# Attention output in token order by transfers, and the softmax denominators by small transfers of their own

## The reference, cut to what matters

```python
out = jnp.einsum('bnqk,bnkh->bnqh', attn, v)      # b, head n, query q, channel h
out = out.reshape(B, -1, S)                       # 256 x 256: the reshape mixes q, h and n
x = x + jnp.einsum('bds,nhd->bsd', out, W_out)    # = out[b, d, s] * sum over n, h of W_out[n, h, d]
```

## Time and profile before

| | |
|---|---|
| median of three runs | 965.46 us (962.29 to 969.97) |
| the profiled execution | 962.93 us |
| its span | 961.2 us |
| mean granted clock of TensorE | 0.967 |
| TensorE busy (PE) | 887.1 us, 92% of the span |
| VectorE, ScalarE, GpSimd busy | 586.2, 487.4, 496.3 us |
| chain that ended last: PE, VectorE, ScalarE, DMA, SP's queue | 80%, 7%, 5%, 2%, 2% |

### The profile page before, as it was taken

How to read it: one execution, slowest core, us unless ns; L and a number is a source line. 1 busy time by engine, 2 the same in 40 slices (tenths; PEclk the granted TensorE clock), 3 DMA queues, 4 the chain that set the end, 5 groups by cost and what they waited for, 6 DMA issues and landing times.

```text
span 961.2 us, 31757 instructions
## 1 busy us (share of the span) xinstructions
PE 887.1 (92%) x11966; PEld 653.0 (68%) x11966; DVE 586.2 (61%) x1292; ACT 487.4 (51%) x839; POOL 496.3 (52%) x705
## 2 busy tenths in 40 slices
PE   5999999999997689899998988999999999999995
PEld 3667667667665356565564776778888888878783
DVE  4856766766764456777777657455555555555552
ACT  3667677677666367566455542333333333333331
POOL 2556666566565333366666667534444434444432
PEclk9999999999999799999888899999999999999998
DMA  9222443443445654455453233433332333233322
GB/s 283 70 57 67 93 129 90 96 127 90 92 119 121 172 183 132 146 177 179 144 162 118 90 86 89 87 62 51 48 51 47 53 49 52 46 52 52 47 34 23
DMA packets 133197, 92.96 MB, mean 97 GB/s; under 512 B 75712, under 2 KB 114112, under 8 KB 132928
## 3 DMA queue, kind: packets, MB, share of 16 engines
q1 hardware_dynamic: 119760, 73.10, 28.2%
q0 software_dynamic: 13296, 17.83, 11.1%
HBM read 54.65 MB, written 37.32 MB: 96 GB/s over the span
## 4 chain that ended last, share of the span: by engine, by line
PE 80%; DVE 7%; ACT 5%; issue 3%; DMA 2%; SPq 2%; another core or an unknown queue 1%; POOL 0%; DVEq 0%; ACTq 0%; POOLq 0%
PE pair L933 19%; PE pair L949 12%; PE pair L951 6%; PE pair L634 5%; PE pair L671 5%; PE pair L657 4%; PE pair L811 3%; PE pair L607 3%; PE pair L684 2%; PE pair L825 2%; PE pair L829 2%; PE pair L861 2%; PE pair L900 2%; PE pair L786 1%; PE pair L837 1%
## 5 line engine op out<-in xcount | busy, mean ns | idle before, releaser
L933 PE MATMUL pair<-XTs,WU 128*128 128x128 bf16 x3408 | 283.9, 219 | 5.9 <-DVE XTs L1269 2.9
L933 PEld LDWEIGHTS pair<-XTs,WU 128*128 x3408 | 238.1, 98 | 71.7 <-issue 8.7
L1603 POOL DMA_INDIRECT out_d<-XB x71 | 116.1, 1635 | 207.4 <-DVE XB L1291 174.0
L949 PE MATMUL pair<-WD,Hh 128*128 x568 | 214.8, 379 | 1.3 <-issue 1.3
L1469 ACT ACTIVATE Hf<-pair 128x512 f32<-128x512 f32 x142 | 84.8, 597 | 219.5 <-PE pair L933 207.9
L1282 DVE CAST Hh<-Hf 128x512 bf16<-128x512 f32 x142 | 64.5, 454 | 172.1 <-ACT Hf L1469 166.9
L951 PE MATMUL pair<-WD,Hl 128*128 x568 | 154.7, 272 | 0.0
L1284 DVE TENSOR_TENSOR Hl<-Hf,Hh 128x512 bf16<-128x512 f32 x142 | 99.5, 701 | 4.9
L1514 POOL TENSOR_SCALAR_AFFINE_SELECT PT<-PT 128x512 f32<-128x512 f32 (+1 forms) x96 | 73.9, 787 | 44.2 <-ACT PT L1320 28.7
L1576 POOL DMA_INDIRECT xs_scr<-XB,WGf x64 | 66.9, 1045 | 31.7 <-issue 18.2
L1488 POOL TENSOR_TENSOR LS<-LS,mhalf 128x2 f32<-128x2 f32 x48 | 34.1, 711 | 94.6 <-DVE LS L976 93.9
(11 more groups left out here) (243 smaller groups left out, 1728.9 us busy)
## 6 DMA issues: line engine op xcount, KB each, us to landing
XB<-xs_scr SPq DMA_DIRECT2D x71, 130.0 KB
STG<-wup_in SPq DMA_DIRECT2D x32, 256.0 KB
q_scr<-SPL SPq DMA_DIRECT2D x16, 512.0 KB, 4.2
STG<-wdn_in SPq DMA_DIRECT2D x32, 256.0 KB
o_scr<-On SPq DMA_DIRECT2D x32, 128.0 KB, 4.2
Mm<-o_scr SPq DMA_DIRECT2D x16, 256.0 KB, 3.0
CnT<-ctxt_in SPq DMA_DIRECT2D x16, 256.0 KB, 4.0
CX<-ctx_in SPq DMA_DIRECT2D x16, 256.0 KB, 4.4
```

The source lines that it names most:

```text
L933: t = e.matmul(upb(j, k)[:, 128 * (fm % 4):128 * (fm % 4) + 128], WU[:, bass.ds(reg[j] * 4096 + off, 128)], XTs[:, r, hx, dk, :], start=n ...
L949: e.matmul(yb[r][:, 0:512], Hh[:, r, hsl], WD[:, bass.ds(reg[i] * 4096 + 512 * fk, 512)], start=fk == 0, stop=False, skip_group_check=True)
L1603: e.indirect_dma_start(out=out, out_offset=bass.IndirectOffsetOnAxis(ap=XS[:, i % NX, 256:257].bitcast(I32), axis=0), in_=Yf[:, i % NY, :] ...
```

## The change

- A4, X1's transposes and their PSUM user go away on TensorE. The projection's heads are laid out anew so that partition group j holds heads 4j to 4j+3 (`places` in layout, `c` in PV).
- ScalarE's copy of PV to OTs now writes the order (s', g, d'), reading PSUM in that permuted order.
- SP (step OT) issues one transfer of the denominators' rows from OTs to a small tile dnc, and four of 16 partitions that write the undivided output to DRAM in token order. XA reads it back, 256 KB, with tokens on partitions.
- VectorE (step RC) takes the reciprocal of dnc and multiplies by wsq. SP (step WB) writes this factor to DRAM with four transfers, and BC reads it back with two, each repeated over the 16 tokens that share it, as XR.
- VectorE (step X1, vector_residual) multiplies XA by XR and adds x.
- The orders change with it: X1 and A6s stand between S1's and S0's maxima on VectorE, A6s behind T0's first masks on GpSimd, and in SP's list the two loads of a round come behind XA.

```diff
 ROUND = {
-    "tensor": "AX:1 MG:1 S1:0:0 T0:1:0 PV:2 S1:0:1 QK:-1 T0:1:1 S0:0 VX:0 T2:1 GT:15 weights:1:2 A4:2",
-    "vector": "Gp:16 weights:-2:0 A6s:4 weights:-1:1 S1:0:1 S0:0 VX:0 A4:2 weights:1:2 MG:0 AX:0 S1:-1:0 Gs:15 A0s:-3",
+    "tensor": "AX:1 MG:1 S1:0:0 T0:1:0 PV:2 S1:0:1 QK:-1 T0:1:1 S0:0 VX:0 T2:1 GT:15 weights:1:2",
+    "vector": "Gp:16 weights:-2:0 weights:-1:1 S1:0:1 X1:4 A6s:4 S0:0 RC:2 weights:1:2 MG:0 AX:0 S1:-1:0 Gs:15 A0s:-3",
     "scalar": "PV:2 A0n:-2 QK:-1 T0:1:1 Gt:13 A6c:4 weights:-2:0 A6n:4 VX:0 T2:1 weights:-1:1 AX:0 GT:15 MG:0 T0:0:0",
-    "gpsimd": "weights:0:2 split:0 T0:1:0 T0:1:1 split:0 GT:15 T2:1 A6c:4 A0s:-3 A6s:3",
-    "sync": "GT:15 load:0 A4:3 AX:1 Go:16 queries:16 decays:16",
+    "gpsimd": "weights:0:2 split:0 T0:1:0 A6s:4 T0:1:1 split:0 GT:15 T2:1 A6c:4 A0s:-3",
+    "sync": "GT:15 BC:3 AX:1 OT:2 WB:2 XA:2 load:0:0 load:0:1 Go:16 queries:16 decays:16",
 }
...
+        def vector_denominators(e, w, b):
+            w.wait_ge(l_dc, 16 * (b + 1))
+            w.wait_ge(l_wb, 64 * b)
+            e.reciprocal(dnc[:, :], dnc[:, :]).then_inc(dvc.sem, dvc.up())
+            w.wait_ge(dvc.sem, dvc.n)
+            e.tensor_tensor(rc[:, :], dnc[:, :], wsq[:, :], ALU.mult).then_inc(rc_.sem, 1)
+
+        def vector_residual(e, w, b):
+            r = b % 2
+            w.wait_ge(l_xa[r], 16 * (b // 2 + 1))
+            w.wait_ge(l_bc, 32 * (b + 1))
+            e.tensor_tensor(XA[:, r, :, :], XA[:, r, :, :], XR[:, :, :], ALU.mult).then_inc(dvc.sem, dvc.up())
+            w.wait_ge(dvc.sem, dvc.n)
+            e.tensor_tensor(xb(b), XA[:, r, :, :], xb(b), ALU.add).then_inc(x1_.sem, 1)
...
                 elif kind == "PV":
                     w.wait_ge(pv.sem, pv.at(b))
-                    w.wait_ge(wsq_, 2)
-                    w.wait_ge(oT.sem, oT.at(b - 1))
-                    e.activation(OTs[:, :, :], pair_of("PV", b)[:, :, :].rearrange("p a (r c) -> p (a r) c", r=2), ACT.Copy).then_inc(ot_.sem, 1)
+                    w.wait_ge(wsq_, 1)
+                    w.wait_ge(l_ot, 64 * b)
+                    w.wait_ge(l_dc, 16 * b)
+                    e.activation(OTs[:, :, :].rearrange("p g c -> p (g c)").rearrange("p (s g d) -> p s g d", s=16, g=4),
+                                 pair_of("PV", b)[:, :, :].rearrange("p a (r d s) -> p s (a r) d", r=2, s=16), ACT.Copy).then_inc(ot_.sem, 1)
...
-                elif kind == "A4":
-                    w.wait_ge(on_.sem, on_.at(b))
+                elif kind == "OT":
+                    w.wait_ge(ot_.sem, ot_.at(b))
+                    w.wait_ge(rc_.sem, rc_.at(b - 1))
+                    e.dma_start(dnc[:, :], OTs[16:128:32, :, :].rearrange("p g c -> p (g c)").rearrange("p (s c) -> p s c", c=32)).then_inc(l_dc, 16)
+                    ov = osc[b, :].rearrange("(s h d) -> h s d", s=16, h=16)
+                    for j in range(4):
+                        e.dma_start(ov[:, :, 64 * j:64 * j + 64], OTs[32 * j:32 * j + 16, :, :].rearrange("p g c -> p (g c)").rearrange(
+                            "p (s c) -> p s c", s=16)).then_inc(l_ot, 16)
+                elif kind == "XA":
+                    w.wait_ge(l_ot, 64 * (b + 1))
+                    w.wait_ge(x1_.sem, x1_.at(b - 2))
+                    e.dma_start(XA[:, b % 2, :, :], osc[b, :].rearrange("(t p d) -> p t d", t=2, p=128)).then_inc(l_xa[b % 2], 16)
+                elif kind == "WB":
+                    w.wait_ge(rc_.sem, rc_.at(b))
+                    for j in range(4):
+                        e.dma_start(rsc[b, :].rearrange("(s j k c) -> j s k c", s=16, j=4, k=2)[j], rc[32 * j:32 * j + 32, :]).then_inc(l_wb, 16)
+                elif kind == "BC":
+                    w.wait_ge(l_wb, 64 * (b + 1))
+                    w.wait_ge(x1_.sem, x1_.at(b - 1))
                     for tt in range(2):
-                        e.dma_start(osc[b, :].rearrange("(n t p h) -> t p n h", n=NH, t=2, h=16)[tt], On[:, tt, :, :]).then_inc(l_o, 16)
-                    if b < B - 1:
-                        merged(e, w, b)
+                        e.dma_start(XR[:, tt, :], rsc[b, 2048 * tt:2048 * tt + 2048].rearrange("(s a d) -> s a d", s=8, a=1).broadcast_to(
+                            [8, 16, 256])).then_inc(l_bc, 16)
...
```

More of the change, by code:

```diff
@@ L74 @@
 ROUND = {
[2 rows of a table removed]
[2 rows of a table added]
     "scalar": "PV:2 A0n:-2 QK:-1 T0:1:1 Gt:13 A6c:4 weights:-2:0 A6n:4 VX:0 T2:1 weights:-1:1 AX:0 GT:15 MG:0 T0:0:0",
[2 rows of a table removed]
[2 rows of a table added]
 }
 LIMITS = {"S1": (0, B - 1), "T0": (0, B - 1), "PV": (0, B - 2), "A0s": (0, B - 1), "A0n": (0, B - 1), "QK": (0, B - 1), "A6s": (0, B - 4),
[L83 removed]
+          "A6n": (0, B - 4), "S0": (0, B - 1), "VX": (0, B - 1), "T2": (0, B - 1), "A6c": (0, B - 4), "X1": (0, B - 4), "OT": (0, B - 2), "XA": (0, B - 2),
+          "RC": (0, B - 2), "WB": (0, B - 2), "BC": (0, B - 2), "AX": (-2, B), "MG": (0, B)}
 def words(line):
@@ L115, in attn_steps @@
     yield "MG", B + 1, 0
-    yield "A4", B - 1, 0
+    yield "OT", B - 1, 0
     yield "contexts", 0, 0
+    yield "queries", 1, 0
+    yield "WB", B - 1, 0
+    yield "XA", B - 1, 0
     yield "decays", 1, 0
-    yield "queries", 1, 0
     yield "contexts", 1, 0
+    yield "BC", B - 1, 0
 def attention_rest():
     z = B - 1
-    return {(0, 0): (("A6s", z - 2), ("Mm", z), ("X1", z - 1), ("A6n", z - 2), ("A6c", z - 2)),
+    return {(0, 0): (("X1", z - 2), ("A6s", z - 2), ("RC", z), ("X1", z - 1), ("A6n", z - 2), ("A6c", z - 2)),
             (0, 1): (("A6s", z - 1), ("XQ", z - 2), ("A6n", z - 1), ("A6c", z - 1)), (0, 2): (("X1", z), ("A6s", z)),
@@ L281, in build @@
         OTs = sb("OTs", [128, 4, 256], F32, ca)
[L282 to L285, removed]
+        dnc = sb("dnc", [128, 32], F32, ca)
+        rc = sb("rc", [128, 32], F32, ca)
+        wsq = sb("wsq", [128, 32], F32, ca)
+        XA = sb("XA", [128, 2, 2, 256], F32, ca)
+        XR = sb("XR", [128, 2, 256], F32, ca)
         QN = sb("QN", [128, 2, 256], F32, ca)
@@ L394, in build @@
         t2m, ex2, pt2 = (sig(n, [(b, u) for b, _ in of(pe_attn, "T2") for u in range(2)]) for n in ("t2m", "ex2", "pt2"))
-        pv, ot_, oT, on_, mT, x1_ = (sig(n, each) for n in ("pv", "ot_", "oT", "on_", "mT", "x1_"))
-        l_o, l_m = sem("l_o"), [sem("l_m0"), sem("l_m1")]
+        pv, ot_, rc_, x1_ = (sig(n, each) for n in ("pv", "ot_", "rc_", "x1_"))
+        l_ot, l_dc, l_wb, l_bc, l_xa = sem("l_ot"), sem("l_dc"), sem("l_wb"), sem("l_bc"), [sem("l_xa0"), sem("l_xa1")]
         qn_, qT, qnh, qnl, ch_, cl_ = (sig(n, each) for n in ("qn_", "qT", "qnh", "qnl", "ch_", "cl_"))
@@ L519, in build @@
         EPS = 5e-5
-        tb_users = [s[:2] for s in pe_steps if s[0] in ("X1", "XQ", "GA", "GT", "GE", "B4", "B5")]
+        tb_users = [s[:2] for s in pe_steps if s[0] in ("XQ", "GA", "GT", "GE", "B4", "B5")]
         def tb_free(w, kind, b):
@@ L677, in tensor_attn @@
                     ps = pair_of("VX", b)
[L678 to L690, removed]
-                        for dk in range(2):
[L692 to L703, removed]
+                    w.wait_ge(wql, 2)
+                    for tt in range(2):
+                        n = 0
+                        for dk in range(2):
+                            for wt, v in ((WQh, xTh), (WQl, xTh), (WQh, xTl)):
+                                t = e.matmul(ps[:, 0, 256 * tt:256 * tt + 256], v[:, b % 2, dk, 128 * tt:128 * tt + 128], wt[:, dk, 512:768],
+                                             start=n == 0, stop=n == 5, skip_group_check=True)
+                                n += 1
+                    t.then_inc(vmm.sem, 1)
                 elif kind == "AX":
@@ L999, in vector_weights @@
             w.wait_ge(wsqm, 1)
[L1000 to L1006, removed]
+            selv = CF[:, C_SEL:C_SEL + 8].rearrange("p (k a) -> p k a", a=1).broadcast_to([128, 8, 32])
+            e.tensor_tensor(wtmp.rearrange("p (k c) -> p k c", c=32), pair_of("weights", 2)[:, 0, 0:256].rearrange("p (k c) -> p k c", c=32),
+                            selv, ALU.mult).then_inc(dvc.sem, dvc.up())
+            w.wait_ge(dvc.sem, dvc.n)
+            e.tensor_reduce(wsq[:, :], wtmp.rearrange("p (k c) -> p c k", c=32), AX.X, ALU.add).then_inc(wsq_, 1)
+            w.wait_ge(wsq_, 1)
+        def vector_denominators(e, w, b):
[9 more added lines that the diff above has]
+            e.tensor_tensor(XA[:, r, :, :], XA[:, r, :, :], XR[:, :, :], ALU.mult).then_inc(dvc.sem, dvc.up())
+            w.wait_ge(dvc.sem, dvc.n)
+            e.tensor_tensor(xb(b), XA[:, r, :, :], xb(b), ALU.add).then_inc(x1_.sem, 1)
         def vector_attn(e, w):
@@ L1030, in vector_attn @@
                                         AX.X, ALU.max, negate=True).then_inc(mx0.sem, 1)
[L1031 to L1045, removed]
+                elif kind == "RC":
+                    vector_denominators(e, w, b)
+                elif kind == "X1":
+                    vector_residual(e, w, b)
                 elif kind == "AX":
```

(9 more changed lines are left out.)

35 lines of the change are left out of this document (9 added, 26 removed).

## The result

The changed kernel takes **1182.16 us** (median of four runs, 1174.97 to 1187.48); the kernel before, on the same chip, 963.88 (median of four, 961.58 to 969.97). The ratio is 1.225, 95% interval 1.216 to 1.234. The forecast said slower, 1125 us and at most 1170: the direction and the place are right, the size is 57 us short. The profiled execution has a span of 1180.9 us, 219.7 more than before's.

The account below looks back on a forecast made before the run. TensorE set the pace before; afterwards a ring over late weight loads would: 12.1 us more in twelve rounds (145), 8.5 in two (17), sum 162 on 962.93, 0.3% under the median: 1125 us, range 1085 to 1170.

Parts of the forecast that it names:

- The removed transposes: TensorE, each round: 1.46 us removed, at most 0.85 us of gain, nothing inside the idle time that opens.
- the ring: Through all five queues, closed once a round over the late weight loads: 12.1 us more per round; chance 0.88.
- VectorE's moved residual and ScalarE's permuted copy: Residual and statistics, 2.7 us, hidden in 3.16 us of VectorE's idle time; ScalarE's permuted PV copy costs zero.
- S0's end to the factor: From S0's end over VectorE's maxima and reciprocal to the product's start: 3.0 us.
- WB and XA: SP's issues ahead of the loads: four factor writes at 0.42 us plus gaps, and one read: 2.3 us.
- The landing: Arrival of the 256 KB weight load, priced at the context transfer's median: 4.0 us (least 2.7, most 5.3).
- Split, masks, roots: GpSimd behind the load: split 1.8 us, two masks 1.2, reciprocal roots 1.3.
- A6n to T0 with the clock: From ScalarE's A6n to TensorE's T0: 5.4 us, plus 0.7 for half clock (bounds 0 to 4.8).
- those 10.50 don't change: The piece of a round from T0 to the end of the next S0 keeps its 10.50 us.
- The tail: Beyond the attention stage: nothing booked, plus or minus 4 us.
- Rival B: Load ring slack; a shorter one binds, context transfer behind BC's wait for X1: some 2 us, twelve rounds, 987; chance 0.04.
- SP waiting for rc: Sign that the prediction is right: SP waits for VectorE's rc, not for GpSimd's split.

Follow-up runs that it names:

- experiment 3: Changed kernel with SP's list as AX, OT, next round's first load, BC, XA, WB, next round's second load: 968.34 us, ratio 1.002 to the kernel before.
- Experiment 2: Changed kernel with OT's five transfers ahead of BC on SP, loads still last: 1155.26 us, ratio 1.195 to the kernel before.
- experiment 9: experiment 3 with SP's gate transfers ahead of XA and WB, and the closing steps' transfers reordered: 963.93 us, ratio 1.001 to the kernel before.
- experiment 1: Changed kernel with the two weight loads of a round back at the head of SP's list: 1032.29 us, ratio 1.067 to the kernel before.
- experiment 6: Changed kernel with 54 unused matmuls ahead of AX's transposes in each round with the second norm: 1198.15 us, ratio 1.239 to the kernel before.
- experiments 7: Changed kernel with 62 unused matmuls ahead of AX's transposes from round 4 on: 1190.87 us, ratio 1.229 to the kernel before.
- experiment 8: Changed kernel with 62 unused matmuls ahead of AX's transposes in rounds 4 to 14 alone: 1175.25 us, ratio 1.213 to the kernel before.

## Why the prediction fell short

By its steps, on the round shown above:

- **The removed transposes**: right. Nothing of them is won while the ring closes; without it 0.76 of the 0.85 us (experiment 3).
- **VectorE's moved residual and ScalarE's permuted copy**: right. X1's product and sum are 0.68 and 0.69 in the idle stretch, and OTs takes 1.02 us.
- **S0's end to the factor: the step that failed.** Predicted 3.0, measured 5.1 (273.79 to 278.91). I let VectorE's reciprocal follow S0's maxima at once, as in the earlier trace rows, where it reads PSUM. In the changed kernel it reads dnc, and dnc comes by a transfer that stands on SP behind BC, which waits for X1 of the same round, and behind AX's two. It is issued at 274.38, and the reciprocal starts 3.95 us later. I had walked SP's list for what the load waits for, and not for what each earlier entry waits for. So the profile's chain of waits goes from X1 over BC and AX to dnc, and not through S0's maxima:

```profile
271.29 0.70 DVE XB L996
...
274.38 3.93 DMA dnc<-OTs
```

A quicker landing of dnc alone would win little: SP was issuing OT's four writes until 278.57 and waited 0.4 us more for the factor, 0.2 to 1.6 in the twelve rounds from 142 us on. BC's wait for X1 holds up both. Experiment 2, which takes all five transfers of OT out from behind it, gives 27 us back; no run parts dnc's landing from the time that SP needs for the writes.
- **WB and XA**: predicted 2.3, measured 3.2 (278.91 to 282.08). One write of the factor takes SP 0.62 us with the gap behind it (2.48 / 4); I had taken the 0.42 of a read of as many partitions.
- **The landing**: predicted 4.0, measured 3.1. Here the row's least of 2.7, which I set aside, was nearer, and so was the 3.0 (median) of the read of Mm in the kernel before, also 256 KB. The 2.6 us estimated from the Trainium skill's page "DMA: Bandwidth & Descriptors" (Anatomy of one DMA), by its fit for the GpSimd path, was nearer than my 4.0 as well, and 0.5 short of the trace.
- **Split, masks, roots**: 4.3 predicted, 4.3 measured (285.18 to 289.51).
- **A6n to T0 with the clock**: 6.1 predicted, 5.8 measured (289.51 to 295.27). But "those 10.50 don't change" was wrong: T0 to S0's end stays 10.5 (263.28 to 273.79) in rounds of 32, and is 12.4 in the one of 34 (295.27 to 307.68), since T0 and PV run below full clock. The upper bound of the clock's term was for this (T0 and PV at the lower level), and I had left it out of the range.
- **Sum**: 21.5 us for 19.7 from S0's end to T0, and 11.6 for 10.5 behind it: 33.1 for 30.2 in eleven rounds, 32 us. By steps that is +2.1, +0.9, -0.9, 0, -0.3 and +1.1 a round: that the issues and the landing cancel is luck, and the failed step is the largest term. Rounds 2 and 3: 29.3 for 26.6, 5 us. The twelfth ring closes through the gates' chain: from S0(15) to T2(15) the shift against before grows from 188.4 to 205.5 us, 17 for 12, 5 us. 32 + 5 + 5 = 42 of the 57.
- **The tail**: booked at 0 plus or minus 4, measured 14 (the shift is 217.1 at the first Hf, less 188.4 and 17.1, and 2.6 more at the end of the span). SP issues one transfer after another from 507 to 544 us there. Experiment 3 gives back the same 14 without any ring, and in experiment 9's profile 3.9 of them are left (8.5 ahead at the last S0, 4.6 at the first Hf), so most of it hangs on the order of SP's issues. That the new transfers of the last two batches are what fills its queue there is argued and not shown.
- **Rival B**: rightly given a small chance, since the longer ring hides it. But its wait of BC for X1 is a part of the longer ring too, by the failed step. Its price of 2 us a round over the 18.1 of before is really 4: 22.3 us on average in experiment 1 ((318.14 - 95.13) / 10, by the first loads).
- **"SP waiting for rc"**: wrong as a sign. SP waits for XB in front of BC, 260.5 us, because an in-order queue shows its wait at the first entry that isn't ready, and by the time that SP comes to WB the factor is nearly there.

## What to carry to other kernels

When transfers are added to an in-order queue, write down for each entry what it waits for, in the order of the list, and carry every wait on to all entries behind it: prefetches go ahead of the first entry that waits for something of the same round. A ring is as long as the sum of its queues' own delays, so price it with the new operand's arrival and not with the old one's. TensorE work removed from a round that waits for a transfer wins nothing while that wait lasts; look for what the freed time will be spent on before you count it.

## What the runs showed of the hardware

- What SP pays to issue a transfer here differs by form: 0.45 us for a weight chunk of 256 KB (median), 0.43 for contexts, 0.59 for a factor's write, 0.79 for a write of 16 partitions of OTs (3.15 / 4), 1.01 for dnc in the round shown, 0.57 in the cheapest round. Sixteen issues fill eleven microseconds of a round (272.06 to 283.02).
- TensorE ran AX at full clock after 54 extra matmuls and 2.4 us of idle time, and T0 and PV, 4.2 and 6.6 us later, below it (experiment 6). With more of them and less idle time it stayed at full clock through most rounds (experiments 7 and 8).
- A round that waits stays long when the waiting engine is kept busy: 30 us of TensorE in 32 (experiment 8) look like a kernel bound by TensorE and are not. Busy time alone didn't tell here who sets the pace.
